# Three row copies per step of a recurrence, written as reductions over an axis of one element

## The reference

```
x = x + L0(_gn(x))        # 1x1 conv, depthwise 3x3, attention inside heads, 1x1 conv
x = x + L1(_gn(x))        # four recurrences over rows and columns

def _conv1d(x, w, b):     # 48 -> 48 channels, 5 taps along the line, zero padded
    return conv(x, w) + b
def f(carry, inp):
    nxt = inp + _conv1d(carry, w, b)
    return (nxt, nxt)
```

## Time and profile before

| what | value |
|---|---|
| median of 3 runs | 11233.95 us (11228.52 to 11236.1) |
| the profiled execution, its own time | 11223.83 us |
| its span, first to last instruction | 11222.2 us |
| mean granted TensorE clock | 0.962 |
| PE busy | 9281.9 us (83%) |
| DVE busy | 9259.9 us (83%) |
| ACT busy | 6164.5 us (55%) |
| POOL busy | 2867.0 us (26%) |

### The profile page before, as it was taken

The page is one execution under the profiler, slowest core; times in us unless marked ns, Lnnn a source line. Parts: engine busy times, 40 slices in busy tenths (PEclk is TensorE's granted clock), DMA queues, the critical chain, the costliest instruction groups (busy, mean ns, idle before and its releaser), DMA issues. The chain is left out here.

```text
span 11222.2 us, 198801 instructions
## 1 busy us (share of the span) xinstructions
PE 9281.9 (83%) x66142; PEld 8313.0 (74%) x66142; DVE 9259.9 (83%) x15547; ACT 6164.5 (55%) x9514; POOL 2867.0 (26%) x2285
## 2 busy tenths in 40 slices
PE   4999999999999999997888888887888888888300
PEld 4999999999999977776777677776777767777200
DVE  8888887777777756668999999999999999999523
ACT  3777777777777744445656544444666654444100
POOL 0000000000000000004555455554555545555100
PEclk9999999999999999999999999999999999999655
DMA  8778776666666679995555456666545546566799
GB/s 259 170 168 170 168 160 131 130 134 132 134 132 134 128 211 293 287 284 144 155 141 153 136 140 152 152 146 151 146 146 157 147 123 156 145 148 156 282 433 408
DMA packets 735867, 2002.99 MB, mean 178 GB/s; under 512 B 59952, under 2 KB 601984, under 8 KB 642016
## 3 DMA queue, kind: packets, MB, share of 16 engines
q1 hardware_dynamic: 591232, 1598.47, 56.7%
q10 hardware_dynamic: 110208, 251.95, 6.3%
q0 software_dynamic: 34304, 151.01, 5.3%
HBM read 1296.36 MB, written 704.64 MB: 178 GB/s over the span
## 5 line engine op out<-in xcount | busy, mean ns | idle before, releaser
L1527 POOL TENSOR_TENSOR lines<-hi,lo 96x512 f32<-96x512 f32 x2048 | 2717.6, 1327 | 2714.2 <-DVE lo L1489 2714.2
L1397 PE MATMUL scan_ps<-lo,scan_high 128*96 128x256 f32 x12264 | 1966.1, 295 | 953.0 <-DVE lo L1489 953.0
L1483 DVE CAST lo<-hi 32x256 fp32r<-32x256 f32 x2048 | 2597.0, 1268 | 63.8
L1559 ACT CAST hi<-scan_ps 96x512 fp32r<-96x512 f32 x2048 | 1192.6, 582 | 2476.5 <-PE scan_ps L1397 2475.4
L1397 PEld LDWEIGHTS scan_ps<-lo,scan_high 128*96 128x96 f32 x12264 | 1481.7, 162 | 1428.5 <-DVE lo L1489 1428.5
L464 PE MATMUL conv_ps<-tap_low,x_high 128*128 128x432 f32 (+2 forms) x6144 | 1908.1, 311 | 0.0
L464 PE MATMUL conv_ps<-tap_high,x_low 128*128 128x432 f32 (+2 forms) x6144 | 1905.8, 310 | 0.0
L464 PE MATMUL conv_ps<-tap_high,x_high 128*128 128x432 f32 (+2 forms) x6144 | 1881.5, 306 | 13.4 <-DVE x_edge L666 7.4
L1489 DVE TENSOR_TENSOR lo<-scan_ps,hi 96x512 fp32r<-96x512 f32 x2048 | 1406.3, 687 | 38.1 <-PE scan_ps L1397 10.4
L1397 PE MATMUL scan_ps<-hi,scan_low 128*96 128x256 f32 x8176 | 1316.3, 283 | 0.0
L1397 PE MATMUL scan_ps<-hi,scan_high 96*96 96x256 f32 x8176 | 1315.5, 283 | 0.0
(11 more groups left out here) (149 smaller groups left out, 12210.0 us busy)
## 6 DMA issues: line engine op xcount, KB each, us to landing
raw<-x SPq DMA_DIRECT2D x764, 256.0 KB, 4.9
v_blocks<-xs ACTq DMA_DIRECT2D x128, 768.0 KB, 4.5
v_in<-v_blocks SPq DMA_DIRECT2D x64, 1536.0 KB, 13.5
d_rows<-lines SPq DMA_DIRECT2D x32, 3072.0 KB, 17.2
u_cols<-lines SPq DMA_DIRECT2D x128, 768.0 KB, 12.0
r_cols<-lines SPq DMA_DIRECT2D x32, 3072.0 KB, 17.0
l_rows<-lines SPq DMA_DIRECT2D x128, 768.0 KB, 12.0
fin_x<-x_scan SPq DMA_DIRECT2D x24, 4096.0 KB, 31.1
```

The source lines that it names most:

```text
L1397: return nc.tensor.matmul(ps[:, k % SLOTS, x], taps[rows, TAPS_OF[way], at], of[rows, x_in, :, shift:shift + LQ], start=False, stop=False, ...
L1483: nc.vector.tensor_copy(spare_of(lo[:, k % LOS], Y), odd_rows(k, 0))
L1527: nc.gpsimd.tensor_tensor(to, high, low, ALU.add).then_inc(state_done, 1)
L1559: nc.scalar.copy(high_of(k), ps[:, k % SLOTS]).then_inc(hi_ready, 1)
```

## The change

The three copies of each step become reductions by maximum over a trailing axis of one element. A maximum of one value is that value, so the same data are written to the same places. Semaphores, waits, order, tiles and engines stay as they are.

```
-    nc.vector.tensor_copy(spare_of(hi[:, k % HIS], X), odd_rows(k, 32)).then_inc(high_spare, 1)
-    nc.vector.tensor_copy(spare_of(lo[:, k % LOS], Y), odd_rows(k, 0))
-    nc.vector.tensor_copy(spare_of(lo[:, k % LOS], X), odd_rows(k, 64))
+    nc.vector.tensor_reduce(spare_of(hi[:, k % HIS], X), odd_rows(k, 32).unsqueeze(3), AX.X, ALU.max).then_inc(high_spare, 1)
+    nc.vector.tensor_reduce(spare_of(lo[:, k % LOS], Y), odd_rows(k, 0).unsqueeze(3), AX.X, ALU.max)
+    nc.vector.tensor_reduce(spare_of(lo[:, k % LOS], X), odd_rows(k, 64).unsqueeze(3), AX.X, ALU.max)
```

## The result

The changed kernel takes **9997.79 us** (median of 4 runs, 9992.75 to 10000.59) against 11235.03 us (4 runs, 11228.52 to 11238.07): a ratio of 0.8899, 95% interval 0.8884 to 0.8914, 1237 us less. The forecast was 10,030 us with a range of 9,950 to 10,200.

What follows compares the result with a forecast made beforehand. VectorE sets the period of the four recurrence passes; 3 x 0.42 + 0.687 + 0.089 = 2.036 us a step from 2.622, 2048 x 0.586 = 1200 us less, gives 10,034 us, said as 10,030; range 9,950 to 10,200.

Steps and rivals of the forecast that it cites:

- L1483's excess is a wait for GpSimd: Middle copy on VectorE: 0.979 of its 1.268 us a step is waiting for GpSimd's addition L1527.
- The reduction costs 0.42: VectorE, three times a step: each 256-element reduction takes 0.42 us by itself, against 0.289 for an unhindered copy.
- The rival of two slots an element (0.69): VectorE's three reductions: each output takes two slots, 0.69 us a reduction, 11,690 us in all; chance 0.05.
- The reduction doesn't wait: VectorE beside GpSimd's addition: reductions do not wait as L1483 did, which gives back 0.979 us a step.
- the slow rate: VectorE: only fast-rate instructions need something GpSimd holds, so a reduction at about 1.04 ns an element does not wait.
- rival of a reduction that waits: VectorE: the reduction waits for GpSimd as the copy does, 3.01 us a step, 12,030 us; chance 0.05.
- The gaps, 0.089 us: VectorE: idle gaps between its four instructions make 0.089 us a step, kept in the new period.
- The prediction's own range: Whole kernel: reductions of 0.41 to 0.43 us and gaps of 0.08 to 0.10 give 9,960 to 10,090 us.
- TensorE second, the rest covered: In the passes: TensorE's 1.91 us a step stays under VectorE's 2.036; ScalarE, GpSimd and transfers do not bound.
- The expected waiting of 0.1 us of TensorE for L1489: TensorE, before the products with the low part: about 0.1 us of waiting left of 0.46 idle.
- The subtraction held up by GpSimd: Rival at L1489: overlaps GpSimd's addition by 0.12 us and waits, period 2.16 us, 10,280 us; chance 0.05.
- Transfers: DMA in the passes: at most 1.58 us a step, not the bound; "left" buffers hold with 5 and 12 us to spare.

Runs made afterwards that it cites:

- the two sizes: Changed kernel plus a fourth reduction per step, 32 x 64 elements: 0.212 us against 0.412 for 256 elements; 10443.02 us, ratio 0.93 to the kernel before.
- The first experiment: Changed kernel with L1482 a copy again, L1483 and L1484 still reductions: 9821.08 us, ratio 0.8748 to the kernel before.

## Why the prediction was right

- **L1483's excess is a wait for GpSimd.** Right, and shown from both sides: shortening the addition removes it; moving the copies in time moves it to L1484 or shrinks it to 1.12 us, and each time the copy ends 0.15 to 0.16 us after the addition.
- **The reduction costs 0.42.** It measured 0.412; three times 0.008 is 0.024 us a step, 49 us in all. The rival of two slots an element (0.69) is refuted by the row and by the two sizes.
- **The reduction doesn't wait.** Right, but the reason given for it, the slow rate, failed: an instruction at the slow rate with two inputs waited and cost 800 us more than the copies. This agrees with the Trainium skill, "SBUF — State Buffer", section "Who interferes with whom", which counts instructions with two SBUF inputs among those that exclude a GpSimd instruction that reads SBUF, and says of a reduction on this chip that it never does. Both halves have rows now: 1.399 us for L1483 with two inputs, at most 0.415 for the reduction. The prediction had the right outcome for the reduction with a property too wide: its own reason gave 10,040 for the two-input rewrite, which came out at 12,037. Its rival of a reduction that waits had been priced at 12,030 from the rows, so the schedule of a waiting instruction was right; only which instruction waits was not.
- **The gaps, 0.089 us.** VectorE stood idle before its four groups for 237.8 us in the changed kernel; the rows give 52.6 of these to waits for ScalarE and TensorE, and the other 185.2 are 0.090 us a step. The earlier trace rows gives 0.090 in the same way. The step is then 3 x 0.412 + 0.686 + 0.090 = 2.012 us against 2.036 forecast, 49 us in all, which is the price above. The profiled execution came out 31 us under its forecast of 10,024, because 12 us more of waits (40.8 before) and 3 us more of the final sum stand against the 49, with 3 in rounding. The median was 32 us under 10,030. The prediction's own range is slightly off: its terms give 9,954 to 10,118, not 9,960 to 10,090; the result lies in either.
- **TensorE second, the rest covered.** Right: taking 0.123 us off VectorE (copy in first place) gained 0.086 us a step, 177 us, and then TensorE stopped it. The expected waiting of 0.1 us of TensorE for L1489 doesn't show as idle time: the page of the profile has 2.4 us idle in all before the products with `lo`. It is there in the spacing. In the step shown the six products start 0.05 us after L1489 ended (the prediction read this distance as 0.03, and its 1.05 us for the next subtraction fits 0.05; nothing hung on it). They take 0.80 us to the next 512-column product (6000.12 to 6000.92), where the stretch in which TensorE waited for nobody has 0.72 (5099.32 to the 5100.04 of the earlier trace rows), and their weight load starts with them rather than 0.12 us ahead of them. The rows of that stretch, from the kernel before:

```profile
5099.20 0.76 PEld L1397 LDWEIGHTS scan_ps<-lo,scan_high 128*96 128x96 f32 x6
5099.32 0.88 PE L1397 MATMUL scan_ps<-lo,scan_high 128*96 128x256 f32 x6
```

- **The subtraction held up by GpSimd.** It is not, but the changed kernel can't show it: both run only from 6001.40 to 6001.51, and an overlap of 0.11 us would not lengthen even an instruction that waits (see the last section). The first experiment can: there L1489 starts at 7002.74 and the addition ends at 7002.96, 0.22 us of overlap, and L1489 has 0.687 us at the median and 0.689 at most. That covers one input from SBUF and one from PSUM up to 0.22 us; a longer overlap wasn't tried. By the estimate of the last section, the prediction's price for this rival, 0.12 us a step, was too high.
- **Transfers.** Right that they stay covered. The median landing of a store in "left" went from 12.0 to 12.7 us and of a load stayed at 16.8; the engines were busy 0.72 of the passes. ScalarE waited for a load 2.1 us in all.

## What to carry to other kernels

When one of several equal VectorE instructions is much longer than its sisters, look at what GpSimd runs just before its end. In these runs a copy between SBUF tiles at the fast rate, or an instruction with two SBUF inputs, and an addition on GpSimd kept each other out. A reduction over an axis of one element is a copy that stays out of this; it costs 1.04 in place of 0.51 ns an element. So use it only for the rows that would collide, and ask which these are after the change: L1484 was unhindered only because L1483 had waited out the addition, and it waited itself once L1483 no longer did (10623 us). The mix of one copy ahead of GpSimd and two reductions behind its start was the fastest of those that compute the whole output (9821 us), while reductions in the two places that did not collide before, with the copy left in the middle, made the kernel slower (11407 us). Ask next which engine is late by how little; here TensorE was 0.1 us behind.

## What the runs showed that was not expected

GpSimd's addition tells from its own length who was ahead of it. It has a median of 1.297 us behind a reduction, 1.327 behind a copy and 1.458 behind a two-input maximum; the instruction in L1482's place, which starts 0.11 us ahead of it, holds it up unless it is a reduction, by 0.03 us (copy) and by 0.16 (two inputs). It is the form of L1482 that counts and not that of L1483: the median is 1.326 and 1.331 in the two mixes with a copy in first place, and 1.292 in the one with a reduction there. The difference between 1.458 and 1.327, 0.131 us, is that between the lengths of L1482 in the two kernels (0.421 and 0.289). The cut addition shows the same step: 0.231 us at the median beside copies, 0.198 beside reductions.

In the other direction, a held instruction ends later than the addition by its own unhindered length less about 0.14 us: 0.15 for the copy of 0.289, 0.28 for the two-input maximum of 0.42. So the two can lie over each other for some 0.14 us at no cost, an estimate from these two rows. A row of the copies with the cut addition agrees: the middle copy starts at 7001.59, 0.03 us before the addition ends (7001.39 + 0.23), and has 0.288 us like its sisters, 0.291 at most. An overlap shorter than 0.14 us says nothing on whether an instruction waits.
